# Running the scores of a three-stage transformer block three units ahead of the transposes instead of two

## What is computed

```python
def attn_a(X, Wq, Wk, Wv, Wpost):                 # X: 16 x 512 x 256, already normalised
    Q = (X @ Wq).reshape(n, s, 16, 64)
    K = (X @ Wk).reshape(n, s, 16, 64)
    V = (X @ Wv).reshape(n, s, 16, 64)
    raw = einsum('bshe,bthe->bsth', Q, K / 8)
    attn = softmax(raw, axis=2)                   # over the 512 keys t
    A = gelu(einsum('bsth,bthe->bshe', attn, V).reshape(n, s, 1024))
    return X + A @ Wpost
x = x + attn_a(layernorm(x), ...)
```

## Time and profile before

| | |
|---|---|
| median of 3 runs | 4303.76 us (4300.8 to 4309.9) |
| the profiled execution | 4303.39 us, of which 4301.6 us are the span from the first to the last instruction |
| busy over the span | TensorE 3881.6 us (90%), VectorE 2600.2, ScalarE 2375.6, GpSimd 1935.2 |
| mean granted TensorE clock | 0.966 of full speed |
| first stage | some 2370 us of the span, up to about 2390 |
| DMA | 315.59 MB, of which most are the stacking transfers of the first stage |

### The profile page before, as it was taken

How to read it: one execution, slowest core, us unless ns; L and a number is a source line. 1 busy time by engine, 2 the same in 40 slices (tenths; PEclk the granted TensorE clock), 3 DMA queues, 4 the chain that set the end, 5 groups by cost and what they waited for, 6 DMA issues and landing times. The chain is left out here.

```text
span 4301.6 us, 65471 instructions
## 1 busy us (share of the span) xinstructions
PE 3881.6 (90%) x23682; PEld 2729.0 (63%) x23682; DVE 2600.2 (60%) x4133; ACT 2375.6 (55%) x4593; POOL 1935.2 (45%) x1227
## 2 busy tenths in 40 slices
PE   6999999999999999999999468999999999999987
PEld 5777777777777777777777344555555555555544
DVE  5666666666666665666666356666666656665652
ACT  3555556555655555556556135555555555555554
POOL 2455445454545554454545343444444444444412
PEclk9999999999999999999999679999999999999998
DMA  4444344434433444444344122222222222222220
GB/s 117 92 100 96 77 99 98 99 89 99 99 91 83 98 98 95 93 99 99 81 93 92 54 44 49 49 49 49 50 51 50 50 50 50 50 50 50 45 41 16
DMA packets 152352, 315.59 MB, mean 73 GB/s; under 512 B 23072, under 2 KB 76704, under 8 KB 152032
## 3 DMA queue, kind: packets, MB, share of 16 engines
q1 hardware_dynamic: 152032, 311.39, 34.2%
HBM read 33.43 MB, written 25.17 MB: 14 GB/s over the span
## 5 line engine op out<-in xcount | busy, mean ns | idle before, releaser
L360 POOL TENSOR_TENSOR e_a<-e_a,recip 128x1024 f32<-128x1024 f32 x512 | 969.5, 1894 | 1114.5 <-DVE recip L566 1114.5
L1099 DVE TENSOR_REDUCE max_b<-ps_s 128x2 f32<-128x1024 f32 x512 | 624.4, 1220 | 328.2 <-PE ps_s L883 326.9
L478 ACT ACTIVATE e_a<-ps_s,neg_max 128x512 f32<-128x512 f32 x1024 | 693.2, 684 | 201.3 <-DVE neg_max L559 198.5
L559 DVE TENSOR_REDUCE neg_max<-ps_s 128x2 f32<-128x1024 f32 x512 | 622.9, 1217 | 278.8 <-PE ps_s L402 278.7
L982 ACT ACTIVATE et<-ps_s 128x1024 f32<-128x1024 f32 x512 | 522.3, 1020 | 352.5 <-PE ps_s L897 350.3
L841 POOL TENSOR_TENSOR h_lo<-h,h_hi 128x512 fp32r<-128x512 f32 x256 | 325.4, 1290 | 481.6 <-ACT h_hi L1018 479.6
L487 ACT ACTIVATE et_a<-ps_t 128x512 f32<-128x512 f32 x346 | 206.3, 596 | 508.5 <-PE ps_t L414 507.7
L430 PE MATMUL ps_o<-et_a,v_a 128*64 128x256 f32 x4096 | 470.3, 382 | 0.0
L401 PE MATMUL ps_s<-stack_a 128*128 128x512 f32 x1024 | 423.8, 414 | 14.4 <-DMA stack_a<-raw_a 14.3
L414 PE MATMUL ps_t<-ident,e_a 128*128 128x128 f32 x2752 | 389.2, 274 | 22.2 <-POOL e_a L360 17.6
L402 PE MATMUL ps_s<-stack_a 128*128 128x512 f32 x1024 | 406.4, 397 | 0.0
(11 more groups left out here) (205 smaller groups left out, 7886.6 us busy)
## 6 DMA issues: line engine op xcount, KB each, us to landing
stack_a<-raw_a SPq DMA_DIRECT2D x256, 384.0 KB, 4.7
stack_a<-raw_a SPq DMA_DIRECT2D x256, 256.0 KB, 4.1
stack_a<-raw_a SPq DMA_DIRECT2D x256, 128.0 KB, 3.6
q_stack<-roped_q SPq DMA_DIRECT2D x256, 64.0 KB
k_stack<-roped_k SPq DMA_DIRECT2D x256, 64.0 KB
x_a<-X SPq DMA_DIRECT2D x16, 512.0 KB, 3.6
X<-x_a SPq DMA_DIRECT2D x16, 512.0 KB, 5.8
x_ahead<-X SPq DMA_DIRECT2D x16, 512.0 KB, 3.9
```

The costliest lines, as they stand in the source:

```text
L360: nc.gpsimd.tensor_tensor(e_a[:, u % 3, :, :], e_a[:, u % 3, :, :], factor, ALU.mult).then_inc(e_normed, 1)
L478: ins = nc.scalar.activation(e_a[:, u % 3, j, :], ps_s[:, 2 * (u % 2) + j, :], ACT.Exp, bias=neg_max[:, u % 4, j:j + 1], accum_out=sums[:, ...
L559: nc.vector.reduce_max(neg_max[:, u % 4, :], ps_s[:, 2 * (u % 2):2 * (u % 2) + 2, :], AX.X, negate=True)\
L1099: nc.vector.reduce_max(max_b[:, u // 4 % 2, :, u % 4], ps_s[:, 0:2, :], AX.X, negate=True)\
```

## The change

Scores, maxima and exponentials of unit k+3 (instead of k+2) are made in slot k, reciprocals and the normalisation of unit k+2 (instead of k+1). The transposes, the copies of what was transposed, the values and all products stay in their slots, and so do the stacking transfers. The exponentials get a fourth place in e_a, which then ends at 206 KB, the end of the arena. `exps(u)` waits for the transposes of unit u-4.

```diff
--- before.py
+++ after.py
@@ -79,7 +79,7 @@
         stack_a = at("stack_a", 130, [P, 2, 2, 3, S], F32R)
         raw_a = at("raw_a", 154, [P, 2, 4, S], F32R)
         et_a = at("et_a", 170, [P, 5, TB, HS])
-        e_a = at("e_a", 190, [P, 3, 2, S])
+        e_a = at("e_a", 190, [P, 4, 2, S])
 
         wa_raw = at("wa_raw", 86, [P, KT, 3 * DA])
         wpost_raw = at("wpost_raw", 110, [P, DA // P, D])
@@ -357,7 +357,7 @@
                 def normalise_exps(u):
                     pool.wait_ge(recip_ready, u + 1)
                     factor = recip[:, u % 4, :].rearrange("p (j o) -> p j o", o=1).to_broadcast([P, 2, S])
-                    nc.gpsimd.tensor_tensor(e_a[:, u % 3, :, :], e_a[:, u % 3, :, :], factor, ALU.mult).then_inc(e_normed, 1)
+                    nc.gpsimd.tensor_tensor(e_a[:, u % 4, :, :], e_a[:, u % 4, :, :], factor, ALU.mult).then_inc(e_normed, 1)
 
                 def heads_low(n):
                     pool.wait_ge(heads_high, n + 1)
@@ -373,8 +373,8 @@
                     nc.gpsimd.tensor_tensor(rstd[:, :], rstd[:, :], minus_half[:, :], ALU.pow).then_inc(rstd_ready, 1)
 
                 for slot in range(FIRST, LAST):
-                    if 0 <= slot + 1 < UNITS_ALL:
-                        normalise_exps(slot + 1)
+                    if 0 <= slot + 2 < UNITS_ALL:
+                        normalise_exps(slot + 2)
                     for n in pairs_at(LOWS, slot):
                         heads_low(n)
                     for s in range(BATCH):
@@ -411,7 +411,7 @@
                         for t in (2 * part, 2 * part + 1):
                             for j in range(2):
                                 c = (t % 2) * HS + j * P
-                                last = nc.tensor.transpose(bank(fill)[:, c:c + P], e_a[:, u % 3, j, t * P:(t + 1) * P], ident[:, :])
+                                last = nc.tensor.transpose(bank(fill)[:, c:c + P], e_a[:, u % 4, j, t * P:(t + 1) * P], ident[:, :])
                         last.then_inc(bank_filled[fill % 3], 1)
 
                 def values(n):
@@ -459,8 +459,8 @@
                     last.then_inc(bank_filled[fill % 3], 1)
 
                 for slot in range(FIRST, LAST):
-                    if 0 <= slot + 2 < UNITS_ALL:
-                        scores(slot + 2)
+                    if 0 <= slot + 3 < UNITS_ALL:
+                        scores(slot + 3)
                     if 0 <= slot < UNITS_ALL:
                         transposes(slot)
                     if slot % 4 == 0 and 1 <= slot // 4 <= PAIRS * BATCH:
@@ -472,10 +472,10 @@
             def _(act):
                 def exps(u):
                     act.wait_ge(max_done, u + 1)
-                    if u >= 3:
-                        wait_filled(act, fill_of["turn", 1, u - 3])
+                    if u >= 4:
+                        wait_filled(act, fill_of["turn", 1, u - 4])
                     for j in range(2):
-                        ins = nc.scalar.activation(e_a[:, u % 3, j, :], ps_s[:, 2 * (u % 2) + j, :], ACT.Exp,
+                        ins = nc.scalar.activation(e_a[:, u % 4, j, :], ps_s[:, 2 * (u % 2) + j, :], ACT.Exp,
                                                    bias=neg_max[:, u % 4, j:j + 1], accum_out=sums[:, u % 4, j:j + 1])
                     ins.then_inc(exp_done, 1)
 
@@ -514,8 +514,8 @@
                         high(todo)
                     if 0 <= slot < UNITS_ALL:
                         copy_turned(slot)
-                    if 0 <= slot + 2 < UNITS_ALL:
-                        exps(slot + 2)
+                    if 0 <= slot + 3 < UNITS_ALL:
+                        exps(slot + 3)
                     for s in range(BATCH):
                         if slot - UNITS * s in GELUS:
                             first = PAIRS * s + 4 * GELUS.index(slot - UNITS * s)
@@ -608,12 +608,12 @@
                     nc.vector.tensor_copy(parts_of(n)[:, 0, :], heads_a[:, n % 6, :]).then_inc(heads_high, 1)
 
                 for slot in range(FIRST, LAST):
-                    if 0 <= slot + 1 < UNITS_ALL:
-                        invert(slot + 1)
+                    if 0 <= slot + 2 < UNITS_ALL:
+                        invert(slot + 2)
                     for todo in todo_of.get(slot - 1, []):
                         low(todo)
-                    if 0 <= slot + 2 < UNITS_ALL:
-                        unit_max(slot + 2)
+                    if 0 <= slot + 3 < UNITS_ALL:
+                        unit_max(slot + 3)
                     if 0 <= slot < UNITS_ALL:
                         copy_turned(slot)
                     if (slot - 1) % 4 == 0 and 1 <= (slot - 1) // 4 <= PAIRS * BATCH:
```

## The result

The changed kernel takes 4484.34 us (median of 4 runs, 4476.97 to 4488.59) against 4302.83 us of the kernel before, a ratio of 1.0417 with a 95% interval from 1.0399 to 1.0435. It is slower by 4.2%; 4478 us had been forecast. The profiled execution took 4488.6 us and has a span of 4486.8 us, 185.2 us more than before, with the same instructions.

What follows compares the result with a forecast made beforehand. TensorE's queue was taken to bound the kernel's first stage. The terms 179 + 6 + 12 - 27.6 - 32.3 - 7.9 + 45 = +174 us on 4303.4 gave 4478 us; range 4400 to 4570 for 8 in 10.

Steps and rivals of the forecast that it cites:

- The stalls: TensorE's scores would wait for each pair's stacking transfers: 179 us over 16 batches, 6 in pair 1.
- The subtraction of issue, landing and today's start of the scores one unit ahead: Pair's new wait on TensorE: last transfer's issue plus landing time minus today's start of scores(4n-1); 11.2 us per batch.
- the eighth batch: Pairs 56 to 63 in the first stage, whose 11.2 us of waits were taken for each of 16 batches.
- Waits on GpSimd, 27.6 us off: TensorE's transposes would no longer wait for GpSimd's normalised exponentials: all 27.6 us removed.
- The 12 us given back before pair 62's stall: With a GpSimd wait gone, TensorE reaches pair 62's stall 0.77 us earlier per batch and waits longer: 12 us.
- The bank wait behind the gelus, -32.3: TensorE's products waiting for VectorE to empty a bank: gone as ScalarE catches up during a stall, between 0 and -32.3 us.
- The clock, +45: First stage: 32 more gaps over 2 us on TensorE at 1.4 us each of lower granted clock, 45 us.
- Two of the signs named for the profile: First stage longer by 170 to 180 us; longest transfer wait over 4 us once per batch, at slot 21.
- Transfers that start earlier: Rival: ScalarE finishes exponentials sooner, so stacking transfers issue up to 0.68 us earlier, saving 56 us: 4422 us; chance 0.09.
- The harder clock: Rival: every TensorE stall over 1 us costs twice 1.4 us, 157 in place of 45, up to 4590; chance 0.07.
- the one that gains by the landing itself: Rival: the stack's last transfer lands 2.9 us after issue, stalls are 44 us in all, 4280 us; chance 0.02.
- the estimate of 2.9 us: Landing time of the 384 KB stacking transfer by the skill's fit, 2.0 us plus bytes over 436 GB/s.

Runs made afterwards that it cites:

- e2: Changed kernel, three units ahead, with scores waiting only for their own head's three transfers, a semaphore for each head: 4295.94 us, ratio 0.9983 to the kernel before.
- e4: Changed kernel with Q and K products, stacking and transposes of x each one slot earlier: 4291.53 us, ratio 0.9974 to the kernel before.
- e9: Kernel before, two units ahead, with Q and K products and the stacking one slot later: 4755.25 us, ratio 1.1051 to the kernel before.

## Why the prediction was right

Point by point, against the profiled execution's +185.2 us of span:

- **The stalls.** Forecast 179 + 6 + 12 with the start-up wait of 6.4 kept, 203 us; measured 200.5 (of it 8.0 at the start). 98 waits were found where 95 to 100 were named: 16 in each of the last six pairs of a batch, one at the start and one in pair 1 (6.6 us for a forecast of 5.9). The subtraction of issue, landing and today's start of the scores one unit ahead could be taken as it stood, because nothing else moved against them. That the eighth batch stood for all was a little coarse: over all pairs of the kernel before, the same subtraction gives 10, 39, 20, 39, 56 and 18 us for the third to the eighth pair of a batch (188 in all with pair 1); measured were 11, 37, 20, 39, 56 and 23. The waits by head (e2) and the products moved earlier (e4) take the loss away with three units still ahead, and the late products (e9) bring one without the third unit: it is this distance, and nothing else of the change costs more than the noise.
- **Waits on GpSimd, 27.6 us off.** Those are gone, but 12.4 us of waits on VectorE's copy stand in their place (0.6 before), and 21.7 where no stall covers them. This term was too large: the transposes had a second condition, the bank, that ended almost as late as the first, and the list of waits before had shown only whichever ended last.
- **The 12 us given back before pair 62's stall.** Wrong: TensorE did not reach that stall earlier, since a wait ahead of it was there still, with another name (0.73 us on the copy at 1252.15). The stall was 3.5 us long in the mean, as the subtraction alone gives, and not 4.4. Without these 12 us the forecast of all stalls is 191 us for the 200.5 measured; 5 of the difference are the last pair of each batch. In the time, the 12 us too many here and the 12 us too much taken off in the term above cancel, which is luck.
- **The bank wait behind the gelus, -32.3.** Gone to 0.4 us under the stall, as forecast, and back in e2 when the stall went.
- **The clock, +45.** TensorE's busy time rose by 41.5 us. The price of 1.4 us per gap over 2 us held roughly: 50 such gaps behind the start for 16 before, 41.5 / 34 = 1.2 us.
- **Together.** 186.2 (stalls, 200.5 - 14.3) - 27.6 + 11.8 - 31.9 + 41.5 = 180 of the 185.2 us; the x transposes wait 10.5 us more than before (L442), and some small waits less. Two of the signs named for the profile failed by a little: the stage became 188 us longer and not 170 to 180, and pair 62's kind of stall was 3.1 to 4.5 us long, over 4 us in one batch alone.
- **The rivals.** Transfers that start earlier are refuted by their issues: SP issues the first of the six 3.83 us after the first matmul of K's product, in the median of both kernels, and from that issue to the last landing it is 9.4 us in both. The harder clock is refuted by the busy time, and the one that gains by the landing itself: 4.2 us at the least, with a median of 4.7 as in the earlier trace rows. With that the estimate of 2.9 us, worked out from the fit in "DMA: Bandwidth & Descriptors", "Anatomy of one DMA — SWDGE (gpsimd) path", of the Trainium skill, is not met in any of the 256 transfers of 384 KB; the fit is for the other issue path.

The rule of the same page of the Trainium skill, section "Rules for kernel authors", to issue a transfer early and wait on it late, is borne out in both directions by the kernels with the products earlier and later.

What the change was good for is a second result. It removes the dependence of the transposes on a late normalisation, but in the kernel's order that was worth nothing, as the equal times of the two kernels that wait by head show. It is worth 19 us once VectorE and ScalarE use the room. Whether it is still worth that in the fastest kernel, with the casts moved, was not run.

## What to carry to other kernels

When one step of a software pipeline is moved ahead, take every input of that step and subtract: where it is ready today minus where the step will then start; a transfer that is hidden today with less than a slot to spare is the new bound. A wait that is taken off a list is only gained if the instruction has no second condition that ends just behind it. And where engines hand work to each other in a ring, an order may only pay when both change: against the kernel that waits by head, VectorE's new order alone cost 3.8% and ScalarE's alone 6.1%, and both together gained 1.2%.

## What was not expected of the hardware

- Short waits hide in busy time: 47 us less busy TensorE between two kernels with the same work and much the same granted clock, where the starts of single matmuls show delays of 0.3 us that no list has.
- Six transfers of 1536 KB together land 9.4 us after the first issue, ten of the same bytes after 9.2, and four of 1024 KB after 6.9. So cutting the transfers finer changed little, and moving fewer bytes, in fewer transfers, did.
- In two kernels with many stalls of over 2 us (the change, up to 4.5 us behind its first two pairs, and the one with late products, up to 7.1) TensorE's busy time rose by 1.2 and 1.6 us for each more. The fastest kernel, without a gap over 1.2 us in its steady part, kept the full clock there. The one with the products earlier has gaps of 1.2 us too, and one of 1.9 us at 2345 us. It was five times at the lower level all the same, 17 us in all, and never behind that longest gap, so the longest gap alone doesn't tell whether the clock falls.
